# The order in which output weights are requested in the last head of an attention block

## The reference

```python
h = _layernorm(x) * (1 + ca) + sa
x = x + ga * attention(h)          # 16 heads of 128, softmax with a causal mask over 2048 rows
h = _layernorm(x) * (1 + cb) + sb
x = x + gb * ffn(h)                # 64 routed experts, 4 per row, and two shared ones
```

## Time and profile before

| what | value |
|---|---|
| median of 3 runs | 2029.73 us (2028.84 to 2031.98) |
| the profiled execution: its own time | 2029.64 us |
| its span | 2027.6 us |
| PE busy | 1935.7 us, 95% of the span |
| DVE busy | 1418.3 us, 70% |
| ACT busy | 1122.8 us, 55% |
| POOL busy | 572.5 us, 28% |
| mean granted clock of PE | 0.987 |

### The profile page before, as it was taken

One profiled execution on the slowest core, in us unless ns is written; L12 is line 12 of the kernel. 1 busy time (PEld: TensorE's weight loads), 2 busy tenths in 40 slices (PEclk: granted clock), 3 DMA queues, 4 the chain that ended last, 5 costly groups with the idle time before them and its releaser, 6 DMA issues.

```text
span 2027.6 us, 33851 instructions
## 1 busy us (share of the span) xinstructions
PE 1935.7 (95%) x9823; PEld 1143.6 (56%) x9825; DVE 1418.3 (70%) x3588; ACT 1122.8 (55%) x1643; POOL 572.5 (28%) x583
## 2 busy tenths in 40 slices
PE   5899999999999999999999999689999999999997
PEld 2444444444444444444444444368877778787786
DVE  5687797797797797797797797646545833333476
ACT  3676776776776676676676686413333144354311
POOL 4531230330330330330330311632000132232265
PEclk8899999999999999999999999799999999999999
DMA  7377777777777777777777777874431098999666
GB/s 241 79 164 176 172 174 176 172 173 176 174 171 176 175 171 176 176 170 176 175 170 176 172 157 161 210 206 143 125 110 32 1 299 283 322 299 306 221 203 186
DMA packets 932181, 366.15 MB, mean 181 GB/s; under 512 B 754800, under 2 KB 885920, under 8 KB 932128
## 3 DMA queue, kind: packets, MB, share of 16 engines
q1 hardware_dynamic: 921888, 331.93, 64.0%
q0 software_dynamic: 10240, 33.56, 5.4%
HBM read 138.86 MB, written 41.94 MB: 89 GB/s over the span
## 4 chain that ended last, share of the span: by engine, by line
PE 72%; DVE 8%; issue 6%; DMA 4%; ACT 3%; POOL 3%; SPq 3%; DVEq 0%; ACTq 0%; POOLq 0%
PE gen L1734 10%; PE gen L1735 10%; PE gen L1736 10%; PE strip L1734 6%; PE strip L1736 6%; PE strip L1735 6%; PE pv L1734 5%; PE pv L1735 5%; PE pv L1736 5%; PE strip L2053 5%; DMA wd_sb<-in_L_ffn_Wd 2%; PE strip L2060 2%; DVE p_lo L1310 2%; SPq L501 2%; DVE exps L1286 1%
## 5 line engine op out<-in xcount | busy, mean ns | idle before, releaser
L955 ACT ACTIVATE exps<-exps,nbias,cols_now 128x128 f32<-128x128 f32 (+15 forms) x256 | 329.8, 1289 | 167.5 <-DVE cmin L1296 165.5
L1310 DVE SCALAR_TENSOR_TENSOR p_lo<-exps,rinv,p_hi 128x512 f16<-128x512 f32 (+3 forms) x256 | 404.9, 1608 | 23.8 <-ACT p_hi L964 23.3
L964 ACT ACTIVATE p_hi<-exps,rinv 128x512 f16<-128x512 f32 (+3 forms) x256 | 333.9, 1352 | 35.1 <-issue 13.7
L1286 DVE TENSOR_SCALAR_CACHE_REDUCE exps<-strip 128x512 f32<-128x512 f32 x384 | 250.9, 687 | 126.5 <-PE strip L1736 123.9
L1734 PE MATMUL strip<-kT_hi,qT_hi 128*128 128x512 f16 (+3 forms) x640 | 221.4, 351 | 28.2 <-DVE kT_lo L1239 16.6
L1734 PE MATMUL pv<-pT,v 128*128 128x512 f16 (+3 forms) x640 | 223.3, 349 | 4.5 <-DMA pT<-p_lo 4.5
L1735 PE MATMUL strip<-kT_lo,qT_hi 128*128 128x512 f16 (+3 forms) x640 | 224.3, 350 | 0.0
L1735 PE MATMUL pv<-pT,v 128*128 128x512 f16 (+3 forms) x640 | 223.3, 349 | 0.0
L1736 PE MATMUL strip<-kT_hi,qT_lo 128*128 128x512 f16 (+3 forms) x640 | 221.7, 350 | 0.0
L1736 PE MATMUL pv<-pT,v 128*128 128x512 f16 (+3 forms) x640 | 219.8, 349 | 0.0
L758 POOL TENSOR_TENSOR wq_f<-wq_f,fac 128x512 f32<-128x512 f32 x15 | 15.6, 1041 | 707.5 <-PE gen L1736 707.5
(11 more groups left out here) (285 smaller groups left out, 4302.1 us busy)
## 6 DMA issues: line engine op xcount, KB each, us to landing
at_dram<-at_f SPq DMA_DIRECT2D x64, 256.0 KB, 2.6
wg_sb<-in_L_ffn_Wg SPq DMA_DIRECT2D x64, 256.0 KB
wu_sb<-in_L_ffn_Wu SPq DMA_DIRECT2D x64, 256.0 KB
wd_sb<-in_L_ffn_Wd SPq DMA_DIRECT2D x64, 256.0 KB
yb_dram<-yb SPq DMA_DIRECT2D x64, 256.0 KB
a_f<-at_dram SPq DMA_DIRECT2D x58, 256.0 KB, 2.8
pT<-p_hi SPq DMA_TRANSPOSE x320, 2.7
pT<-p_lo SPq DMA_TRANSPOSE x320, 2.8
```

The source lines that it names most:

```text
L955: nc.scalar.activation(row, row, ACT.Exp, bias=nbias[:, t:t + 1], scale=cols_now[:, LOGIT_UP:LOGIT_UP + 1], accum_out=rsum[:, t:t + 1]).th ...
L964: nc.scalar.activation(p_hi16[:, 0:j + 1, t, :], row, ACT.Copy, scale=rinv[:, t:t + 1]).then_inc(p_hi, 1)
L1286: nc.vector.tensor_scalar(exps[:, t, 512 * ch:512 * ch + w], strip[u % STRIPS][:, 0:w], 1.0, None, ALU.mult, ALU.max, accum_out=cmax[:, t, ...
L1310: nc.vector.scalar_tensor_tensor(p_lo16[:, 0:j + 1, t, :], row, rinv[:, t:t + 1], p_hi16[:, 0:j + 1, t, :], ALU.mult, ALU.subtract).then_i ...
```

## The change

Only SP's program changes: sixteen loads of output weights stay sixteen, but stand at other places. Three now come ahead of the second stage's first transposes, two between that stage's first and last ones, three behind the turning of the third stage's values, two between the third stage's first and last transposes, and three ahead of the six a_early loads; of the last three, one stands behind those six, one behind the fourth stage's first transposes, and one behind the two a_f loads that follow.

```diff
--- before.py
+++ after.py
@@ -560,21 +560,24 @@
                     sp.wait_ge(wo_split, hd - WOS + 1)
                 sp.dma_start(wo_raw(hd), O_w[hd]).then_inc(wo_landed[hd % WOS], 16)
 
+            for hd in range(3):
+                load_wo(hd)
             turn_first_rows(H - 1, 1)
+            for hd in range(3, 5):
+                load_wo(hd)
             turn_last_rows(H - 1, 1)
-            for hd in range(6):
-                load_wo(hd)
             store_at(H - 1, 0)
             turn_values(H - 1, 2, H - 1)
-            for hd in range(6, 9):
+            for hd in range(5, 8):
                 load_wo(hd)
             turn_first_rows(H - 1, 2)
-            for hd in range(9, 12):
+            for hd in range(8, 10):
                 load_wo(hd)
             turn_last_rows(H - 1, 2)
             store_at(H - 1, 1)
             turn_values(H - 1, 3, H - 1)
-            load_wo(12)
+            for hd in range(10, 13):
+                load_wo(hd)
 
             at_parts = at_dram.rearrange("(n h) p s -> n p h s", h=HH)
 
@@ -617,12 +620,13 @@
             sp.wait_ge(at_stored, 16 * (QB * h + 2))
             for u in range(EARLY):
                 load_a(u)
-            for hd in range(13, H):
-                load_wo(hd)
+            load_wo(13)
             turn_first_rows(h, j)
+            load_wo(14)
             sp.wait_ge(strip_done, NSTRIP * H)
             for u in range(EARLY, EARLY + AFS):
                 load_a(u)
+            load_wo(15)
             turn_last_rows(h, j)
             store_at(h, QB - 2)
             sp.wait_ge(wo_split, H - 1)
```

## The result

The changed kernel took 2019.74 us (median of five runs, 2016.75 to 2023.01), against 2029.73 before (2028.84 to 2031.98): a ratio of 0.9952 (95% interval 0.9938 to 0.9966). That is 10.0 us or 0.5% faster, 0.3 us from the forecast of 2019.4. The execution that was profiled is the slowest of the five, 2023.01 with a span of 2021.2. It is 6.6 us shorter than the one before (2029.64), so it must be read in two pieces: the last head, and what lies behind it.

A forecast was written before the change was run, and what follows sets the result against it. PE bounds the kernel, with last-head waits traced to SP standing before POOL's splits. Gains 11.6 + 2.0 less 3.0 made 10.6, taken as 10.2: 2029.64 - 10.2 = 2019.4 us, range 2012.5 to 2027.

The forecast's parts named there:

- Three requests, POOL 17 us earlier: Second stage's gap: heads 0 to 2 issued from about 1240.8 while SP is idle; POOL starts about 1243.8, 17.1 us earlier.
- POOL beside DVE, 2.4 us: Second stage: POOL's splits lengthen DVE's four p_lo, a loss of 2.4 us at the third stage's start; bounds 0 and 5.7.
- it has no cover: Start of third stage: the 2.4 us loss passes to PE's wait for kT_lo, 0.42 us becoming 2.8.
- The second stage's last transposes and the store: Transposes end about 1259.3, store goes out about 1259.4 instead of 1271.62; ACT's wait of 5.19 us goes.
- The third stage's p_lo: DVE's four p_lo, with POOL again beside them and 2.4 us later, end at about 1274.6.
- PE's start of the fourth stage's scores: PE starts at 1276.1 instead of 1277.86, gaining 1.8 us, and about 1 more because it should stay at full clock.
- The transposes of the third stage: Last one issued at 1282.6; ACT's fourth-stage p_hi starts at 1286.2, 12.8 us earlier; PE's 4.46 us wait for pT goes.
- The output projection: After the fourth stage's p_hi chain, PE starts it at about 1296.9, 11.6 us earlier.
- it stands for 2 us instead of 5.08 and keeps its clock: 2.0 us gained: Output projection's start: after a shorter stop PE does its first ten matmuls in 2.2 us instead of 4.2.
- Heads 14 and 15, 3.0 us: Output projection: their weights are split at 1308.4 and 1310.3, after PE asks; loss 3.0 us, bounds 0 and 8.
- Behind it the chain has nothing tied to absolute time: Behind the first row tile, fourth-stage transposes, sums, store, residual rows and reloads move along, so the 10.2 us gain carries through.
- Slower: Rival: heads 8 and 9 wait for POOL, holding third-stage last transposes, if POOL needs over 6.5 us a head; chance 0.05.

The follow-up runs named there:

- zeroed kernel: The change with POOL writing zeros for heads 0 to 2 instead of casting and subtracting, leaving three heads out of the output projection: 2021.46 us.
- kernel with the tail of before: The change, but with heads 13, 14 and 15 all directly behind the six a_early reloads, as before the change: 2023.12 us, ratio 0.9955.
- repetition: The change run again unaltered, against the kernel before: 2020.58 us, ratio 0.9951.
- third profile: Profile of the change unaltered, run a third time in a later session against the kernel before: 2019.64 us, ratio 0.9953.

## Why the prediction was right

- **Three requests, POOL 17 us earlier.** Predicted 1240.8 and 1243.8, measured 1241.06 and 1244.34. That this is the main part is shown by the kernel with it alone: 7.9 of 11.1 us in the medians, 8.4 of 11.0 at last wo.
- **POOL beside DVE, 2.4 us.** Measured 2.1 on DVE and 2.04 on PE's wait (0.42 to 2.46). The Trainium skill, page "SBUF — State Buffer", section "Who interferes with whom", says that a VectorE instruction with two SBUF inputs contends with GpSimd instructions that read SBUF, not with one that only writes it. The zeroed kernel agrees as far as it goes, with a p_lo at 1.28 beside the last two writes of 0.52 us. The 5.7 of the upper bound could not come: the first head's two instructions were over at 1246.31, before the first p_lo began. But "it has no cover" was said too surely. Heads 3 and 4 were a second limit beside it, and taking the contention away gave no earlier p_hi in the one run of it; the kernel with the tail of before speaks for some of it passing through. How much of the 2.1 reaches the end stays open.
- **The second stage's last transposes and the store.** Predicted end 1259.3 and 1259.4, measured 1260.8 and 1260.88; one transpose took 2.65 to issue instead of about 1.3. ACT's wait of 5.19 went, as forecast.
- **The third stage's p_lo.** The end came out, 1274.4 for 1274.6, by errors that cancel. The sum itself had slipped: before, they end at 1272.76, and 2.4 later is 1275.2. They began 3.7 later than before (1265.71, not 1262.00), not 2.4: here behind the exponentials of a slow PE, in the repetition behind the second limit; and they took 7.70 us (1.82, 1.90, and 3.98 for two), not 10.03. POOL was not idle meanwhile: it split heads 5 and 6 from 1266.12 to 1275.57, and its four instructions took 1.88, 2.66, 2.14 and 2.66. Here POOL bore the loss, in the third profile DVE did (9.07 for the four). What decides between them is not shown.
- **PE's start of the fourth stage's scores.** Predicted 1276.1; the three profiles of the change have kT_lo's wait end at 1276.84 and 1275.70 or find kT_lo there. The remark that PE keeps its clock there held where it had lost it at 1255 and so had hardly a wait (1.00 behind 0.56 us at 1275.7), and not in the repetition (0.59 behind 2.88).
- **The transposes of the third stage.** Last issued 1282.72 for 1282.6, p_hi at 1286.79 for 1286.2: 12.2 us earlier for 12.8. Head 9 made SP wait for a microsecond, which I had named as a sign of being wrong; it was too short to matter, and absent in the two later profiles.
- **The output projection.** Started at 1297.47 for 1296.9. The step that failed is **"it stands for 2 us instead of 5.08 and keeps its clock: 2.0 us gained"**. It stood 4.81 us here; but even with 2.17 and, in the second run of the kernel with the last two heads sooner, 1.95 us, the window behind showed 0.59 and 0.65. In all fourteen profiles, that of before among them, the 4.2 us behind this start are at 0.50 to 0.65, behind stops from 1.94 to 8.40 us. My reason was the row of 1366.5 to 1371.0, with 1.55 us of idle time at 1.00. That was no licence for 2 us behind a stage with other idle time in it. In the profiled execution the low clock even lasted longer: 40 matmuls in the first 12.0 us against 44 before, some 0.9 us lost, and behind the stop for the late heads it fell again (0.77, as above).
- **Heads 14 and 15, 3.0 us.** 1.86 in the first profile, 2.65 and 1.63 in the two others: over-sized by 0.4 to 1.4 us.
- **"Behind it the chain has nothing tied to absolute time".** Not so: with the transposes no longer behind heads 14 and 15, PE's later waits fell from 3.39 + 0.20 + 1.55 to 0.98 + 1.57, 2.6 us gained. The kernel with the old tail shows them back, at 1.53 and 4.00.

The sum by what was measured, first profile: 11.0 at the output projection, less 1.9 for the late heads, less 1.1 for the clock, and 2.6 from the later waits, is 10.6, as read. The 1.1 is PE's busy time from there to the row of 1371.87, 69.5 us for 288 matmuls, before 68.4 for as many. I had 11.6 + 2.0 - 3.0 = 10.6. The total is right, two terms in it are not: 2.0 of clock that never came, and 2.6 of waits that I had left out. That they nearly cancel is luck, and so is a forecast within 0.3 us where the sessions' medians say 9.3 to 11.1; the 11 us at the output projection are not.

No rival happened. Slower needed 6.5 us a head on POOL; from 1244.34 to the end of the seventh split, 1275.57, it took 4.5 a head, waits for data included, so that SP stood in front of head 9 for at most one microsecond. That a stand can come back is shown by the kernels with heads 3 and 4 moved, where it was in front of heads 6 and 7.

## What to carry to other kernels

A request that must wait for another engine's work holds everything behind it in its queue; put the ones that need nothing into a gap of the queue early, and the waits of the later ones shrink with them, which here gave three quarters of the gain. Before a contention is charged to the end time, look for a second limit beside it, and test by removing each and both. And once the large stands are gone, look at all waits behind them again: moving requests may be worth nothing where they stand now and 3 us once something else has moved, as the tail was.

## What the runs showed of the hardware

- The granted clock of PE fell behind some waits of about 2.5 us and not behind others of the same length at the same place: 0.57 at 1255.3 after 2.46 us in the first profile and after 2.48 us (at 1254.5) in the third, but 1.00 after 2.40 in the repetition and after 2.57 in the kernel with heads 8 and 9 moved. It fell to 0.80 over 15.6 us at 1512 as well in the first profile, behind stops of 1.14 and 1.61 us that were the same in executions at 1.00; from the second stop to the first matmul on xb it took 112.8 us there, and 110.0 in the other two profiles of the change and before.
- A transpose's issue on SP's queue is not a constant: mostly 1.24 to 1.31 us, but 2.65 and 2.19 in the change, and 3.80 in the zeroed kernel at 1255.16. The 2.65 and the 3.80 came 2 to 4 us behind two requests of weights, the 2.19 (at 1282.72) 7 us behind the last one; what makes them long is not shown.
- DVE and POOL stretch each other where POOL casts or subtracts: 1.28 us for a 128x1024 p_lo became 1.59 to 2.04, while POOL's subtraction of 1.28 became 2.14 and its cast of 0.61 became 1.61. Which of the two pays differs from one profile of the same order to the next: 7.21 us for the four p_lo in the first, 6.23 in that of the kernel with the tail of before.
